# Second cross-attention tile quantised and multiplied ahead of the first FFN transpose, with the rounding of x1 done by a conversion to 8-bit codes

## What is computed

```python
x = x + attention(layernorm(x))          # 4-bit weights, rotary, causal, 32 heads
x = x + cross(layernorm(x), ctx)         # both operands rounded to 256 levels
x = x + layernorm(x) @ binarized(weight).T

def fake_quant(x, scale, zp):
    q = jnp.clip(jnp.round(x / scale + zp), 0.0, 255.0)
    return (q - zp) * scale
def cross(x1, x2, ...):
    return jnp.matmul(fake_quant(x1, ...), fake_quant(x2, ...))
```

## Time and profile before

| | |
|---|---|
| median of 3 runs | 1073.74 us (1073.23 to 1074.12) |
| the profiled execution | 1073.24 us, its span 1071.4 us |
| PE busy | 1030.9 us, 96% of the span |
| DVE, POOL, ACT busy | 935.7 us (87%), 768.7 us (72%), 706.3 us (66%) |
| PE in 950 to 960 us of the span | busy 6.56 of 10 us, mean clock 0.83 |
| PE from 990 to 1067 us | busy 76.73 of 77 us |

### The profile page before, as it was taken

The page is one execution under the profiler, slowest core; times in us unless marked ns, Lnnn a source line. Parts: engine busy times, 40 slices in busy tenths (PEclk is TensorE's granted clock), DMA queues, the critical chain, the costliest instruction groups (busy, mean ns, idle before and its releaser), DMA issues.

```text
span 1071.4 us, 18946 instructions
## 1 busy us (share of the span) xinstructions
PE 1030.9 (96%) x5356; PEld 505.7 (47%) x5356; DVE 935.7 (87%) x1741; ACT 706.3 (66%) x1557; POOL 768.7 (72%) x817
## 2 busy tenths in 40 slices
PE   5999998999999999999999999999999998989998
PEld 3444443444555455455545554544544453444443
DVE  7988998799888888888888889999999999878873
ACT  5547757777777777777777777767776776463320
POOL 4678887888778787777878778988988898332100
PEclk9999999999999999999999999999999999999999
DMA  9774303679767766766776666777777666423543
GB/s 341 245 191 129 112 22 80 148 153 162 163 164 152 162 154 160 150 163 159 155 152 158 161 147 153 157 148 155 165 158 149 151 127 130 114 91 64 99 104 78
DMA packets 309827, 156.13 MB, mean 146 GB/s; under 512 B 257728, under 2 KB 270400, under 8 KB 309728
## 3 DMA queue, kind: packets, MB, share of 16 engines
q1 hardware_dynamic: 301952, 141.69, 57.9%
q10 hardware_dynamic: 7776, 13.37, 4.5%
HBM read 89.20 MB, written 4.19 MB: 87 GB/s over the span
## 4 chain that ended last, share of the span: by engine, by line
PE 38%; POOL 35%; issue 11%; DVE 9%; ACT 5%; DMA 1%; ACTq 0%; POOLq 0%; DVEq 0%; SPq 0%
POOL w_b L1647 10%; POOL prob L1640 8%; POOL swapped L1635 5%; PE proj_ps L1107 5%; POOL q_sb L1660 3%; PE side_ps L929 3%; PE proj_ps L949 3%; PE out_ps L949 3%; PE side_ps L743 3%; PE side_ps L745 3%; PE side_ps L744 3%; POOL rot L1655 3%; PE proj_ps L1112 2%; PE score_ps L1078 2%; DVE rot L2007 2%
## 5 line engine op out<-in xcount | busy, mean ns | idle before, releaser
L1647 POOL TENSOR_TENSOR w_b<-prob,w_b 128x896 f16<-128x896 f32 (+2 forms) x192 | 188.3, 995 | 62.5 <-ACT w_b L1327 62.3
L1640 POOL TENSOR_SCALAR prob<-prob,row_inv 128x512 f32<-128x512 f32 (+3 forms) x256 | 177.9, 705 | 61.9 <-DVE row_inv L2180 59.0
L1300 ACT ACTIVATE prob<-score_ps,neg_max 128x512 f32<-128x512 f32 (+3 forms) x256 | 132.5, 520 | 78.3 <-DVE neg_max L2078 74.6
L743 PE MATMUL side_ps<-hT,w_a 128*128 128x512 f16 x444 | 168.3, 379 | 0.0
L744 PE MATMUL side_ps<-hT,w_a 128*128 128x512 f16 x444 | 168.3, 379 | 0.0
L745 PE MATMUL side_ps<-hT,w_a 128*128 128x512 f16 x444 | 168.3, 379 | 0.0
L2102 DVE SCALAR_TENSOR_TENSOR x_acc<-out_ps,o_now,x_acc 128x1024 f32<-128x1024 f32 x120 | 153.2, 1277 | 0.0
L2102 DVE SCALAR_TENSOR_TENSOR x_acc<-proj_ps,o_now,x_acc 128x1024 f32<-128x1024 f32 x120 | 152.8, 1273 | 0.0
L949 PE MATMUL proj_ps<-work,w_b 128*128 128x512 f16 x496 | 127.3, 379 | 4.3 <-issue 2.3
L949 PE MATMUL out_ps<-work,w_b 128*128 128x512 f16 x496 | 127.3, 379 | 0.9 <-DVE x_acc L2102 0.8
L2078 DVE CUSTOM_DVE_ANT_0 score_ps<-score_ps,mask_b 128x512 f32<-128x512 f32 (+3 forms) x256 | 122.2, 498 | 1.9 <-PE score_ps L912 0.9
(11 more groups left out here) (269 smaller groups left out, 2169.0 us busy)
## 6 DMA issues: line engine op xcount, KB each, us to landing
stage_c<-in_codes_dram SPq DMA_DIRECT2D x72, 256.0 KB, 2.8
stage_o<-in_codes_dram SPq DMA_DIRECT2D x64, 256.0 KB, 2.9
stage_s<-in_scales_dram SPq DMA_DIRECT2D x64, 256.0 KB, 3.4
ctx_raw<-in_ctx_dram ACTq DMA_DIRECT2D x32, 256.0 KB, 3.3
work<-w_b SPq DMA_TRANSPOSE x261, 3.0
x_acc<-in_x_dram SPq DMA_DIRECT2D x8, 512.0 KB, 8.5
k_sb<-in_codes_dram SPq DMA_DIRECT2D x16, 256.0 KB, 6.7
v_sb<-in_scales_dram SPq DMA_DIRECT2D x16, 256.0 KB, 7.0
```

The lines of the kernel that those rows point to most:

```text
L743: pe.matmul(o, stat(0), mov(0), start=first, stop=False)
L1300: ins = act.activation(prob[:, SCORE_AT[qb]:SCORE_AT[qb] + w], score_ps[:, score_bank(i, u), off:off + w], ACT.Exp, bias=neg_max[:, c:c + ...
L1640: return pool.tensor_scalar(prob[:, at:at + w], prob[:, at:at + w], row_inv[:, col:col + 1], P_UP, ALU.mult, ALU.mult)
L1647: ins = pool.tensor_tensor(prob16[:, 1, to:to + w], prob[:, at:at + w], prob16[:, 0, to:to + w], ALU.subtract)
```

## The change

Rounding: `x1_scale` now writes 8-bit unsigned integers (`x1_codes`, the first quarter of the same buffer), so that the conversion rounds and clips. `x1_sum` reads them, with a bias of -128. `x1_quant`, `x1_clip` and `x1_round` are gone, and with them `x1_clip(2)`, which stood on POOL ahead of `x1_add(3)`. Order: tile 1's statistics, roots, norm, scale and sum move ahead of `x2_part(0)` on DVE and of `y_copy(4)` on ACT; on PE `turn_i1(1)` and `cross(1)` come ahead of `turn_h3(0)`, whose eight transposes stand between matmuls 12 and 13 of `cross(1)`.

```diff
 PE
+        def x1_codes(t):
+            return xn[t % 2][:, 0:D // 4].bitcast(U8)
-                        if t == 0 and k == 3:
-                            turn_i1(h + 1)
+                        if (t, h, k) == (0, 1, 0):
+                            turn_i1(2)
-                    if t == 0 and h == 0:
-                        cross(1)
...
             cross(0)
-            for t in range(TB, TT):
-                turn_y(t)
+            turn_y(4)
+            turn_y(5)
+            turn_i1(1)
+            turn_y(6)
+            turn_y(7)
+            cross(1, (0,))
+            cross(1, (1,), range(0, 4))
+            turn_h3(0)
+            cross(1, (1,), range(4, KB))
 ACT
-            def x1_round(t):
-                act.wait_ge(x1_clipped, t - 1)
-                act.activation(xn[t % 2], xn[t % 2], ACT.Copy, bias=ROUND).then_inc(x1_rounded, 1)
-                act.activation(xn[t % 2], xn[t % 2], ACT.Identity, scale=scal[:, 4:5],
+                act.activation(x1_codes(t), xn[t % 2], ACT.Identity, scale=scal[:, 4:5],
-                act.activation(i1[:, t % 2, :], xn[t % 2], ACT.Copy, bias=0.0 if t < 2 else -(ROUND + Q_MID),
+                act.activation(i1[:, t % 2, :], x1_codes(t), ACT.Copy, bias=-Q_MID,
...
             x1_scale(0)
+            x1_sum(0)
             column_part(1, 1)
-            x1_sum(0)
             i1_T_part(0)
             for u in LATE_UNITS:
                 o_scale(u)
+            next_roots(1, 2)
+            x1_scale(1)
+            x1_sum(1)
             y_copy(4)
             y_copy(5)
-            next_roots(3)
+            i1_T_part(1)
+            next_roots(2)
             y_copy(6)
             y_copy(7)
 POOL
                 if t == 2:
-                    pool.wait_ge(x1_shifted, 1)
+                    pool.wait_ge(x1_scaled, 1)
...
             for k in LATE_UNITS:
                 late_add(k)
-            x1_clip(2)
-            x1_add(3)
-            for t in range(4, TT):
+            for t in range(3, TT):
                 x1_add(t)
-                x1_clip(t - 1)
-            x1_clip(TT - 1)
 DVE
             x1_norm(0, 0)
             add_two(1, 0)
-            x1_quant(0)
+            last = x1_stats(2, 1)
             add_two(1, 1)
-            x1_stats(1, 1)
-            add_two(1, 2)
+            row_roots(1, last, 2, lambda: add_two(1, 2))
+            x1_norm(1, 2)
             dve.wait_ge(cc_ready, B * NB)
-            x2_part(0, lambda: x1_stats(2, 2))
-            row_roots(3, row_stats(0, 0))
+            x2_part(0, lambda: x1_stats(1, 2))
+            row_roots(2, row_stats(0, 0))
             h3_norm(0)
...
                 if t == 0:
-                    x1_norm(1, 1)
                     h3_lo(t)
-                    x1_norm(2, 2)
-                    x1_quant(1)
+                    x1_norm(2, 1)
```

More of the change, by code:

```diff
@@ L33 @@
 Q_MID = 128.0
-ROUND = 1.5 * 2.0 ** 23
 H_UP = 2.0 ** 10
@@ L493, in build @@
         x1_scaled = sem("x1_scaled")
-        x1_shifted = sem("x1_shifted")
-        x1_clipped = sem("x1_clipped")
-        x1_rounded = sem("x1_rounded")
         i1_ready = sem("i1_ready")
@@ L1065, in turn_i1, with cross @@
                 mm.then_inc(i1_turned, 1)
-            def cross(t, halves=range(NB)):
+            def cross(t, halves=range(NB), ks=range(KB)):
                 b = t // TB
@@ L1074, in cross @@
                 for h in halves:
-                    if t >= 1:
+                    if t >= 1 and ks[0] == 0:
                         pe.wait_ge(x2_ready, 2 * t - 1 + h)
-                    for k in range(KB):
+                    for k in ks:
                         mm = pe.matmul(score_ps[:, h, :], i1_T[:, t % 2, k, :],
@@ L1080, in cross @@
                                        start=(k == 0), stop=(k == KB - 1))
-                    mm.then_inc(xat_done, 1)
+                    if ks[-1] == KB - 1:
+                        mm.then_inc(xat_done, 1)
             def turn_h3(t):
@@ L1162, in _ @@
                     cross(t + 1)
-                if t < H3_BY_PE:
+                if 0 < t < H3_BY_PE:
                     turn_h3(t)
@@ L1527, in y_copy @@
                     .then_inc(y_copied, 1)
-            def x1_round(t):
-                act.wait_ge(x1_clipped, t - 1)
-                act.activation(xn[t % 2], xn[t % 2], ACT.Copy, bias=ROUND).then_inc(x1_rounded, 1)
             def x1_scale(t):
                 act.wait_ge(x1_normed, t + 1)
-                act.activation(xn[t % 2], xn[t % 2], ACT.Identity, scale=scal[:, 4:5],
+                act.activation(x1_codes(t), xn[t % 2], ACT.Identity, scale=scal[:, 4:5],
                                bias=scal[:, 1:2]).then_inc(x1_scaled, 1)
             def x1_sum(t):
[L1541 to L1544, removed]
+                act.wait_ge(x1_scaled, t + 1)
                 if t == 0:
@@ L1608, in _ @@
                 more = t + 2 < TT
-                if 0 < t < I1_BY_PE - 1:
-                    i1_T_part(t + 1)
                 if t:
@@ L1614, in _ @@
                     h3_high(t)
-                if t == 0:
+                if t < H3_BY_PE:
                     h3_part(t)
-                    x1_scale(1)
                 if more:
                     x1_scale(t + 2)
[L1620 to L1627, removed]
                     x1_sum(t + 2)
+                if 0 < t + 2 < I1_BY_PE:
+                    i1_T_part(t + 2)
         @block.gpsimd
@@ L1779, in x1_add @@
                 if t == 2:
-                    pool.wait_ge(x1_shifted, 1)
+                    pool.wait_ge(x1_scaled, 1)
                 pool.tensor_tensor(x1_rows(t), x1_rows(t), by_block(xs[:, t, :]), ALU.add).then_inc(x1_ready, 1)
-            def x1_clip(t):
-                pool.wait_ge(x1_scaled, t + 1)
-                pool.tensor_scalar(xn[t % 2], xn[t % 2], QMAX, 0.0, ALU.min, ALU.max).then_inc(x1_clipped, 1)
             def late_add(k):
@@ L2218, in x1_norm @@
                 normalise(by_block(xn[t % 2]), x1_rows(t), c).then_inc(x1_normed, 1)
[L2220 to L2224, removed]
             def x2_part(t, between=lambda: None):
```

## The result

The changed kernel takes 1078.81 us (median of 5 runs, 1077.54 to 1079.03) against 1073.74; the ratio is 1.0045, with a 95% interval of 1.0034 to 1.0055. It is slower by 5.1 us, inside the stated range, and 2.1 us beyond the number predicted. The profiled execution has a span of 1077.2 us, against 1071.4.

What follows compares the result with a forecast made beforehand. PE bounds the last tiles, so the start of `dense(0)`, set by `h3_norm(0)`, decides. Courses with clock gave +2.2 to +4.5 us; +3.0 on 1073.24 gave 1076.2, the median 0.5 above: 1076.7 us, range 1070.8 to 1079.4.

Steps and rivals of the forecast that it cites:

- Where the end is decided: Tail: PE work after `dense(1)` begins (976.61 us) is fixed, so what counts is how far that start moves.
- the figure of the sum: PE work left from `dense(0)` to `dense(1)` in the new order: 10.35 + 3.45 + 0.45 = 14.25 us.
- The sum up to h3_norm(0): DVE's chain from tile 0 to the end of `h3_norm(0)`, with POOL's holds: 963.4 or 961.7 us, break-even 960.0.
- Course (a): DVE gets x2's second pass before POOL's `x1_add(4)`: `h3_norm(0)` ends at 963.4, end moves +3.3 us, +4.5 with clock.
- (b): POOL's `x1_add(4)` beats DVE's second x2 pass: `h3_norm(0)` ends at 961.7, end moves +1.7 us, +2.2 with clock.
- the row at 58.15: Earlier trace: a normalisation 0.06 us ahead of POOL still took 2.73 us; read as starting first not securing the operand path.
- The clock: PE at half clock after idling, around `dense(0)`: adds 0 to 1.7 us, taken as 1.2 or 0.5 by course.
- The rounding: `x1_scale` into 8 bits takes 1.25 us; shorter chain pulls `turn_i1(0)` to 940.15, worth nothing for tiles 3 to 7.
- The rival that ended faster: POOL's additions do not hold DVE's chain: 1071 to 1072 us with two holds, 1067.0 with none; chance 0.16.
- the computed chain: DVE's chain with nothing disturbing it: `h3_norm(0)` ends near 953.3, `dense(0)` starts at 955.7, end moves -6.7 us.

Runs made afterwards that it cites:

- e8: The changed kernel with unused spare matmuls in PE's waits, 16 ahead of `turn_i1(1)` and 28 ahead of `turn_h3(0)`: 1076.67 us, ratio 1.003.
- e1: The changed kernel with POOL's additions of tiles 3 to 7 held back by waits on the h3 chain, the first for `h3_norm(0)`: 1069.54 us, ratio 0.9955.
- e4: The kernel before, old rounding and order elsewhere, with only POOL's additions of tiles 3 to 7 put ahead of all `x1_clip`s: 1081.14 us, ratio 1.007.
- e7: The changed kernel with only POOL's additions of tiles 6 and 7 held back until `h3_norm(0)` is done: 1072.72 us, ratio 0.9989.
- e5: The changed kernel with 16 unused spare matmuls ahead of `turn_i1(1)` and 16 ahead of `turn_h3(0)`: 1077.70 us, ratio 1.0037.
- e9_root_first_free: e2_roots_first without the wait in its POOL loop, so the additions of tiles 3 to 7 run free: 1074.04 us, ratio 1.0006.
- e6: The order of e2_roots_first with the kernel before's rounding on DVE, POOL and ACT: 1071.11 us, ratio 0.9974 to the kernel before.
- e3: The kernel before with only the rounding by 8-bit conversion, order and release of POOL's additions as before: 1073.45 us, ratio 0.9999.
- e2_roots_first: As e1, plus tile 1's root ahead of `i1_T_part(0)` on ACT and `add_two(1, 2)` behind tile 1's norm on DVE: 1066.97 us, ratio 0.9936.

## Why the prediction came out as it did

- **Where the end is decided.** Right. After `dense(1)` starts, the rest takes 94.8 us before (976.61 to the end of the span) and 94.6 after (982.65 to 1077.2). The start moved by 6.04 us, 4.57 of it in the tail. That PE alone sets the pace from `dense(0)` on holds too: no DMA wait is left, and at full clock `dense(1)` starts 14.25 us after `dense(0)` (e8), the figure of the sum.
- **The sum up to h3_norm(0).** Course (a), nearly to the tenth. Less the 1.47 us of late start, `turn_i1(0)` is at 940.19 (forecast 940.15), the norm of tile 1 at 948.23 (forecast 948.2), the addition of tile 3 at 945.44 (945.43), and `h3_norm(0)` ends at 963.4 (963.4). The holds are those named: `late_add` and tile 3's addition on the first root, tile 4's on L1813, tiles 5, 6 and 7 on the second. e1 and e4 show from both sides that POOL's additions are the cause, e7 shows the price of one. One reading was loose: the earlier trace rows shows three holds, not four; the fourth, of 1.959 us, stands in the earlier trace rows.
- **The term that was mis-sized.** The choice between courses (a) and (b), which I put at +3.0, "a little toward (b)". It was (a): DVE's second pass of x2 started at 953.91, POOL's addition at 953.96, and the pass ran in 0.75 us. (a) with its clock was +4.5; the tail measured +4.3 to +4.6. I had let the row at 58.15 decide, a norm that began 0.06 us first and was held; a pass that adds two SBUF operands was not held with 0.05. Neither is chance of one run: the pass took 0.75 us in all four profiles where it began 0.04 or 0.05 us first (after, e5, e7, e8), and the norm at 58 us, 0.06 us first, took 2.73 or 2.74 us instead of 0.81 in all eleven. So a start of a few hundredths ahead is enough for one kind of operation and not for the other; why stays open. The Trainium skill's page "SBUF — State Buffer", section "Who interferes with whom", has the first to issue take the port pair; this pass agrees with it, the row at 58.15 still doesn't. In the other close cases POOL was first, by 0.04 us in e4_adds_early and 0.03 in e9_root_first_free, and the norm was held, as page and course (b) both have it.
- **The rest of the difference.** 5.07 us between the medians against 4.3 to 4.6 in the tail. The profiled execution lost 0.9 us in the half clock at 911 us; one was there at 903 in e1_adds_late and at 911 in e4_adds_early too, and none near that place in the other eight profiles. A stretch more or less is enough to move a run by about 1 us: beside e8, the five runs of the kernel before with a mean clock of 0.994 took 1074.25 to 1074.90 us, the other twelve (0.997 or 0.998) 1072.59 to 1074.24. Whether the change makes such stretches any more frequent stays open: nothing before the tail was changed.
- **The clock.** Right: 1.2 us for course (a), inside 0 to 1.7; the profile of e8 gives 1.3 on the path.
- **The rounding.** In the change it costs nothing, as said. That nothing speaks for a gain beyond tile 0 was wrong for the new order: there tile 1's chain stands on the path, and the conversion is worth some 4 us (e6). In the old order no gain was measured at all (e3).
- **The rival that ended faster** fails for the kernel as it is, but its mechanism was real: with POOL out of the way the chain is worth what was computed for it undisturbed, 6.7 us. e2_roots_first shows 6.5, with tile 1's root moved ahead of `late_add` as well, which the computed chain did not need; e1_adds_late, in the changed kernel's own order, shows 3.9.

## What to carry to other kernels

Before a wait or an instruction of a helper engine is removed, ask what it kept apart. Here `x1_clip(2)`, a clip that nobody seemed to need, was also what kept five additions of 2.35 us out of VectorE's critical chain; it has to be replaced by a wait that says so. Where GpSimd works beside VectorE, its work off the critical path is not free. Place it beside VectorE's statistics and the operations that read PSUM: in the profile before, two statistics at 945.54 took 1.27 us and L2236 at 944.87 took 0.75 us beside `late_add`, as long as without it. For each VectorE operation with two SBUF operands, and for each tensor_scalar from SBUF to SBUF of more than one column, that a GpSimd instruction can meet, count up to the whole length of that instruction; one instruction held one such operation here.

## What the hardware showed beyond expectation

- A chain of dependent tiny operations is the worst partner for a queue of long ones. With POOL back to back, VectorE gets one such operation through for each POOL instruction: 2.27, 2.27 us in a row for work of 0.16. The victim was tiny or large alike. A tensor_scalar of 128x1 was never held: L1830 at 934.09 took 0.15 us in the middle of an addition. Each of the eleven profiles has two of that size that began while a POOL instruction ran, and all took 0.15 us. One of 128x2 was held (961.54: 2.27 us).
- POOL itself hardly lost in these meetings with tiny operations. Four additions took 9.82 us against 4 x 2.35 = 9.4. The first, which met VectorE's second pass of x2, took 2.92; the others took 2.33 to 2.35. Where large operations wait in a row both sides pay: in e4_adds_early the additions that met a large operation took 2.78 to 2.80 us, and the passes and norms ended 0.55 us after POOL's end, not with it.
- Filling PE's wait with spare matmuls kept the full clock in the run that left 0.30 us of it (E 1.3 us shorter). In the one that left 2.88 us the clock was at half again from 962.97, and E was 0.4 us shorter.
